# An expert stage written out step by step, with the weight folding spread over the stage before it

## The reference

```python
# attn: 16 heads of 8
q, k, v = xr @ Wq.T, xr @ Wk.T, xr @ Wv.T          # xr = xn by heads
probs = softmax((q * k).sum(-1) / sqrt(128), axis=0)   # over the 16 sequences
attn = probs[..., None] * v.sum(axis=1)[:, None]
# ffn: 16 experts of width 176, top 2, and a shared one of width 352
cw = top-2 weights of softmax(xf @ gate_w + gate_b)
h, g = xf @ w1 + b1, xf @ w3 + b3                  # per expert
y = (silu(h) * g) @ w2, weighted by cw, + cw @ b2
z = silu(xf @ sw1 + sb1) * (xf @ sw3 + sb3) @ sw2 + sb2
out = x + attn + y + z
```

## Time and profile before

| | us |
|---|---|
| median of 3 runs (range) | 261.24 (260.04 to 261.77) |
| the profiled execution | 261.67 |
| its span on the engines | 259.8 |
| first and last scatter to `xslot` start | 34.5, 116.7 |
| first fold of the weights | 109.2 |
| last copy of a fold starts | 126.8 |
| first expert matmul | 129.84 |
| first and last scatter to `ydram` start | 135.60, 236.84 |

### The profile page before, as it was taken

How to read it: one execution, slowest core, us unless ns; L and a number is a source line. 1 busy time by engine, 2 the same in 40 slices (tenths; PEclk the granted TensorE clock), 3 DMA queues, 4 the chain that set the end, 5 groups by cost and what they waited for, 6 DMA issues and landing times.

```text
span 259.8 us, 5535 instructions
## 1 busy us (share of the span) xinstructions
PE 216.3 (83%) x1284; PEld 170.1 (65%) x1285; DVE 185.7 (71%) x525; ACT 115.0 (44%) x331; POOL 151.3 (58%) x170
## 2 busy tenths in 40 slices
PE   0669996799999999999599999999999999990000
PEld 0459943279676655652189999899999999980000
DVE  4898998768765797825747777677777777760495
ACT  2233532831216332224346767676676767750000
POOL 8134058777777777771017777777776777774000
PEclk9999997999999999999979999999999999997555
DMA  5999501446111111110322434343333333311998
GB/s 178 348 383 338 121 29 61 146 141 225 64 58 57 59 57 57 57 59 23 80 57 87 109 112 113 96 116 114 101 110 96 115 109 107 96 51 42 288 395 288
DMA packets 29463, 33.37 MB, mean 128 GB/s; under 512 B 5683, under 2 KB 24627, under 8 KB 29091
## 3 DMA queue, kind: packets, MB, share of 16 engines
q1 hardware_dynamic: 22566, 21.17, 27.9%
q0 software_dynamic: 4576, 9.91, 10.3%
q10 hardware_dynamic: 2304, 2.10, 2.3%
HBM read 18.84 MB, written 14.32 MB: 128 GB/s over the span
## 4 chain that ended last, share of the span: by engine, by line
PE 76%; DVE 8%; DMA 6%; ACT 3%; SPq 3%; issue 2%; POOL 1%; POOLq 0%; ACTq 0%
PE PS L997 15%; PE PS L1016 14%; PE PS L899 8%; PE PS L867 6%; PE PS L868 6%; PE PS L878 4%; PE PS L837 4%; PE PS L1006 4%; PE PS L991 4%; DMA xnT<-ydram 4%; PE PS L1007 3%; SPq L344 3%; PE PS L855 3%; PE PS L830 2%; DVE st L432 2%
## 5 line engine op out<-in xcount | busy, mean ns | idle before, releaser
L419 POOL DMA_INDIRECT ydram<-fw x79 | 75.7, 958 | 44.4 <-DVE fw L703 27.4
L411 POOL DMA_INDIRECT xslot<-XR,idx x64 | 63.5, 993 | 29.5 <-issue 18.0
L1016 PE MATMUL PS<-fw 89*128 (+1 forms) x316 | 49.3, 278 | 0.1
L1016 PEld LDWEIGHTS PS<-fw 89*128 89x128 f32 (+1 forms) x316 | 41.8, 192 | 0.8 <-issue 0.3
L695 DVE TENSOR_TENSOR prod<-prod,PS 128x176 f32<-128x176 f32 x79 | 26.7, 338 | 21.3 <-ACT prod L805 20.8
L805 ACT ACTIVATE prod<-PS 128x176 f32<-128x176 f32 x79 | 25.1, 317 | 18.5 <-PE PS L997 17.9
L997 PE MATMUL PS<-w13h,rxh 128*128 x79 | 32.6, 413 | 0.7 <-DVE rxl L690 0.7
L810 ACT ACTIVATE fw<-PS 88x256 f32<-88x256 f32 x79 | 30.1, 380 | 1.4 <-PE PS L1007 1.0
L703 DVE TENSOR_SCALAR fw<-PS,fw 128x128 f32<-128x128 f32 x79 | 27.7, 350 | 2.8 <-PE PS L1016 2.4
L800 ACT ACTIVATE rxh<-PS 128x128 fp32r<-128x128 f32 x79 | 21.9, 278 | 16.5 <-PE PS L991 16.5
L766 ACT ACTIVATE sS<-PS,sbc 128x512 f32<-128x512 f32 (+1 forms) x18 | 12.2, 686 | 37.5 <-PE PS L868 31.9
(11 more groups left out here) (135 smaller groups left out, 347.0 us busy)
## 6 DMA issues: line engine op xcount, KB each, us to landing
fw<-xslot SPq DMA_DIRECT2D x79, 72.0 KB
fw<-in_w SPq DMA_DIRECT2D x1, 2816.0 KB, 16.0
X<-in_x SPq DMA_DIRECT2D x4, 512.0 KB, 6.2
XR<-ydram SPq DMA_DIRECT2D x8, 256.0 KB, 5.4
out<-X ACTq DMA_DIRECT2D x16, 128.0 KB, 5.3
xnT<-ydram SPq DMA_DIRECT2D x8, 256.0 KB, 7.9
fw<-in_w SPq DMA_DIRECT2D x1, 1536.0 KB, 18.7
ydram<-fw POOLq DMA_INDIRECT x79, 2.2
```

The source lines that it names most:

```text
L411: pool.indirect_dma_start(xslot, bass.IndirectOffsetOnAxis(ap=idx[:, k, t:t + 1], axis=0), XR[:, t, :], None).then_inc(d_sc[k][h], 16)
L419: pool.indirect_dma_start(ydram, bass.IndirectOffsetOnAxis(ap=RX[:, v, TOK:TOK + 1].bitcast(I32), axis=0), yb[:, v, :], None).then_inc(d_y ...
L1016: ins = pe.matmul(PS[:, 6 + b, 0:P], raT[0:n, b, k * P:(k + 1) * P], w2[0:n, bass.ds(e * 2 * P + k * P, P)], start=(k == 0), stop=(k == 1))
```

## The change

Four parts.

1. **Expert steps written out.** `steps` calls `run(j)` for `j` from -1 to 82 on PE, ACT, DVE and POOL. No loop is left there; SP's loads stay a loop.
2. **Folding spread.** The folds move from the end of stage 2 into it, one between two pieces of the shared expert, from after `down(2)` to before `down(5)`. All use bank 5, and each waits for the split of the one before. Their copies (`high`) and splits are put between the `gates` and `gated_up` calls of ACT and DVE. `down` of every group but 1 now writes bank 4 and waits for the `add_z` before it. ACT's wait for the zero fill moves with the first copy.
3. **Bias rows by DMA.** The fold is one matmul of 127 useful rows. The bias row is row 127 (it was row 0; `XR` has its column of ones behind the features instead of ahead). ACT rounds the biases to `bhi`, DVE subtracts to `blo`, SP stores both to DRAM and loads them as row 127 of `w13h` and `w13l`. POOL's five operations that cut the bias in three, and its two for `sel`, go.
4. **Sooner slot loads, other paces.** `KEPT` goes from 8 to 4, and the scatters of the second half wait by new numbers and by a table for folds (`PACE_W`).

The diff, cut to its core (renumbered slices, semaphore names and removed `fixed` arguments left out):

```diff
-WBANK = (0, 2, 1, 3)
-KEPT = 8
+KEPT = 4
+RAW = 8
+WP = P - 1
-PACE_UP = {8: 3, 11: 4, ..., 33: 12, 37: 13, 39: 14, 43: 15, 44: 16, 45: 17, 49: 18, ..., 60: 24}
+PACE_UP = {8: 3, 11: 4, ..., 33: 12, 38: 13, 40: 14, 48: 16, 50: 17, 58: 19, 60: 20}
-PACE_Z = {21: 1, 25: 2, 36: 3, 41: 4, 48: 5, 54: 6, 62: 7}
+PACE_W = {37: 1, 39: 2, 41: 3, 44: 4, 46: 5, 49: 6, 51: 7, 54: 8, 56: 9, 59: 10, 61: 11}
+PACE_Z = {21: 1, 25: 2, 36: 3, 43: 4, 53: 5, 63: 6}
...
-        def steps(eng, run, top=None):
-            turns = (NS - 4) // UN
-            for j in range(-1, 3 + UN):
-                run(j, j, True)
-            with eng.Fori(1, turns) as it:
...
-                for u in range(3, 3 + UN):
-                    run(it * UN + u, u, False)
-            for j in range(3 + turns * UN, NS + 4):
-                run(j, j, True)
+        def steps(run):
+            for j in range(-1, NS + 4):
+                run(j)
...                                                 # SP
-            for k in range(3):
-                sp.dma_start(bdram[k]..., bprt[:, k, :]).then_inc(d_bst, 16)
-            sp.wait_ge(d_bst, 48)
-            sp.dma_start(bsp[:], bdram[:, :]).then_inc(d_bup, 16)
+            for k, part in enumerate((bhi, blo)):
+                sp.dma_start(bdram[k]..., part[:].bitcast(F32)).then_inc(d_bst, 16)
...
+            sp.wait_ge(d_bst, 32)
+            sp.wait_ge(d_fill, 16 + 16 * NE)
+            sp.dma_start(w13h[WP:P, :].bitcast(F32), bdram[0:1, :]).then_inc(d_bup, 16)
+            sp.wait_ge(s_sm, 2 * NB)
+            sp.dma_start(w13l[WP:P, :].bitcast(F32), bdram[1:2, :]).then_inc(d_bup, 16)
...                                                 # ACT, after the copies of group 2
+                    act.wait_ge(l_b, 16)
+                    act.activation(bhi[:], braw[:], ACT.Copy).then_inc(k_bh, 1)
...                                                 # DVE, after norm(7)
+            dve.tensor_tensor(blo[:], braw[:], bhi[:].bitcast(F32), ALU.subtract).then_inc(k_bl, 1)
...                                                 # PE
             def fold(q):
-                if q < 4:
-                    pe.wait_ge(s_sm, NG * NB - 1 + q // 2)
-                else:
-                    pe.wait_ge(s_wl, q - 3)
-                at = PS[:, WBANK[q % 4], 0:WQ]
-                pe.matmul(at, kc[:, K_FOLD:K_FOLD + P], w13[:, cols], start=True, stop=False)
-                pe.matmul(at, sel[:], bsp[:, cols], start=False, stop=True).then_inc(s_w, 1)
+                if q:
+                    pe.wait_ge(s_wl, q)
+                else:
+                    pe.wait_ge(l_w13, 16)
+                    pe.wait_ge(s_za, 2)
+                pe.matmul(PS[:, 5, 0:WQ], kc[:, K_FOLD:K_FOLD + P], w13[:, q * WQ:(q + 1) * WQ],
+                          start=True, stop=True).then_inc(s_w, 1)
             def down(g):
                 if g >= 2:
-                    pe.wait_ge(s_za, g - 1)
+                    pe.wait_ge(s_za, g if g > 2 else 1)
...
```

More of the change, by code:

```diff
@@ L420, in run @@
                                             yb[:, v, :], None).then_inc(d_y[v], 16)
-            steps(pool, run)
+            steps(run)
         @block.vector
@@ L646, in _ @@
             score(7)
+            split(0)
+            shift_scores()
             gated_up(4, 0)
-            shift_scores()
+            split(1)
+            add_z(2)
             gated_up(4, 1)
-            add_z(2)
+            split(2)
+            shares()
+            split(3)
+            add_z(3)
             gated_up(4, 2)
-            shares()
-            add_z(3)
+            split(4)
+            attend(0, True)
             gated_up(5, 0)
-            attend(0, True)
+            split(5)
@@ L656, in _ @@
             gated_up(5, 1)
+            split(6)
             attend(1, True)
+            split(7)
+            add_z(4)
             gated_up(5, 2)
-            add_z(4)
+            split(8)
             attend(2, True)
             gated_up(6, 0)
+            split(9)
+            gated_up(6, 1)
+            split(10)
             attend(3, True)
-            gated_up(6, 1)
+            add_z(5)
             attend(4, True)
             gated_up(6, 2)
-            add_z(5)
+            attend(5, True)
@@ L788, in _ @@
                     gates(g, c)
             act.wait_ge(d_fill, 16 + 16 * NE)
-            for q in range(NW):
-                act.wait_ge(s_w, q + 1)
-                act.activation(w13h[:, q * WQ:(q + 1) * WQ], PS[:, WBANK[q % 4], 0:WQ], ACT.Copy).then_inc(s_wh, 1)
-            def run(j, u, fixed):
-                if has(j + 1, fixed):
-                    b = (u + 1) % 2
+            high(0)
+            act.wait_ge(s_z, 3)
+            gates(4, 0)
+            high(1)
+            act.wait_ge(s_ds, 1)
@@ new lines, in _ @@
+            act.activation(pr[:].rearrange("p c r -> p (c r)"), sd[:].rearrange("p c r -> p (c r)"), ACT.Exp,
+                           scale=float(P) ** -0.5).then_inc(s_exa, 1)
+            gates(4, 1)
+            high(2)
+            high(3)
+            gates(4, 2)
+            high(4)
+            act.wait_ge(s_z, 4)
+            gates(5, 0)
+            high(5)
+            gates(5, 1)
+            high(6)
+            high(7)
+            gates(5, 2)
+            high(8)
+            act.wait_ge(s_z, 5)
@@ L798, in run @@
+            gates(6, 0)
+            high(9)
+            gates(6, 1)
+            high(10)
+            gates(6, 2)
+            act.wait_ge(s_z, 6)
+            for c in range(NB):
+                gates(7, c)
+            def run(j):
+                if has(j + 1):
+                    b = (j + 1) % 2
                     act.wait_ge(r_tp, j + 2)
-                    act.wait_ge(r_up, max(j, 0) if fixed else j)
+                    act.wait_ge(r_up, max(j, 0))
                     act.activation(rxh[:, b, :], PS[:, b, 0:P], ACT.Copy).then_inc(r_xh, 1)
-                if has(j, fixed):
-                    b = u % 2
+                if has(j):
+                    b = j % 2
@@ L810, in run @@
                     act.activation(raT[0:FH, b, :], PS[0:FH, 4 + b, 0:2 * P], ACT.Copy).then_inc(r_att, 1)
             act.wait_ge(k_r1, 1)
-            steps(act, run)
+            steps(run)
             for c in range(NC):
@@ L1020, in _ @@
             read_expert(0, 0)
-            steps(pe, run)
+            steps(run)
 def constants():
```

197 lines of the change are left out of this document (92 added, 105 removed).

## The result

The changed kernel takes 253.26 us (median of 4 runs, 252.61 to 254.27), the kernel before 260.99 (4 runs, 260.04 to 261.77). The ratio is 0.971, 95% interval 0.967 to 0.975. The prediction was 253.5 us.

A forecast was written before the change was run, and what follows sets the result against it. PE and POOL were taken to bound the expert loop at once, so the last scatter plus an untouched tail sets the time. 261.67 - 4.3 - 1.3 - 2.6 = 253.5 us, range 251.0 to 257.0.

The forecast's parts named there:

- Term 1, folds and start-up: First fold to first expert matmul: PE's 20.7 us become 16.4 with one-matmul folds spread out, 4.3 us sooner.
- waits of folds for splits: In the shared expert, PE's waits between folds for the split before: 2.2 us, between 0 and 5.6.
- That leaves over 4 us for the first load.: Expert-stage start: last scatter to xslot lands at 119.0, PE's first transpose comes at about 124.4, so slot loads are in time.
- The rival of the scatter stream: POOL's 64 scatters to xslot stretch by over 4 us, slot loads come 1 to 3 us late: 254.5 to 256.5; chance 0.05.
- Term 2, the clock: Head of the expert stage: granted clock stays full instead of 0.50 for 3.4 us, worth 1.3 us, between 0 and 1.66.
- Term 3, the turns: Expert loop: writing out the steps removes POOL's extra idle time at five loop turns, 2.6 us sooner, between 0 and 2.7.
- The clock did not fall at the start-up: Rival: clock falls all the same, as holes of 0.9 us around down(7) might count together; 254.8 us, chance 0.15.
- ACT and DVE did not bind: Rival: ACT and DVE bound the shared expert, which grows by 5.6 us in place of 2.2; 256.9 us, chance 0.10.
- the turns were the cause: Rival said they were not: a loss only coinciding with expert-loop turns stays, 0.5 us goes; 255.6 us, chance 0.07.
- Code: Rival: PE starves for code in the written-out steps, some 8 more packets, 9.6 us lost; 263 us, chance 0.03.
- the tail: From the last scatter at 236.84 to the end at 261.67: 24.8 us, which the change does not touch.
- The edits at nothing: Bias operations off POOL, rounding and subtraction on ACT and DVE, SP's bias loads, ACT's moved zero-fill wait: no cost or gain.

The follow-up runs named there:

- the version with filler: Written-out steps, one-matmul folds at the end, attend(7) ahead of the last splits, unused matmuls in PE's two long idle times: 252.29 us, 0.967 of the kernel before.

## Why the prediction was right, and where it was right by luck

**Term 1, folds and start-up: -4.3 forecast, -4.82 measured.** Of it 0.60 came from ahead of the folds and 4.22 from the work that the term is about: 23.51 + 29.10 us before, 8.05 + 40.34 after. In detail (forecast, measured): folds 9.5, 9.5; waits of folds for splits 2.2, 1.8 (40.34 - 29.10 - 9.46); hole before `down(7)` 0.9, 1.0; `down(7)` to the first expert matmul 1.1, 1.7. The last is 0.5 over because of the step that failed:

**"That leaves over 4 us for the first load."** It left none. The sum was made with the last scatter starting at 116.7 as before; it started at 118.75 and had landed at 121.01. SP's first load went out at 121.87, and the two transposes started 2.85 and 3.61 us after the landing, where PE was free after 2.35. The 2 us are a start later by 1.07 and a scatter of 2.39 us, neither an effect of the new paces: with the loop kept, the same paces have the last scatter at 115.75, and with `down(7)` in bank 5 at 116.37. But the scatter of 2.39 us is no accident of one execution. It is in eight of the fourteen traces, at the same place of the stream, 13.9 us after its start; here it is in the kernel before with its steps written out:

```profile
48.27 2.39 POOL L402 DMA_INDIRECT xslot<-XR,idx  x1 [0.30 <-issue]
```

All eight are among the nine traces in which the clock stays at 1.00 at 42 us; none of the five in which it falls has it. The gain at 42 us and this loss on POOL mostly come together. In the change the slow scatter stands beside three DVE operations on `sS` (L544, 48.84 to 50.71), as one of 1.30 us at 53.46 does (52.63 to 54.52); whether they hold it isn't shown. The rival of the scatter stream thus came true in a small part, 0.5 us of the 1 to 3 that I gave it. A margin taken from one execution was less sure than the durations taken from it. With the hole before `down(7)` gone and the loads in time, the same piece is 1.3 us (123.19 to 124.49), near the 1.1 forecast.

**What the 0.6 us beyond the term are: luck.** Two effects that I did not have work against each other ahead of the folds. A part of the input landed later, which puts POOL's first scatter and PE behind it 1.07 us later, and the clock did not fall at 42 us:

```profile
43.15 0.27 PE L856 MATMUL PS<-mbf,lbf 128*128 128x256 bf16 x1 [1.29 <-DVE cum L495]
```

PE's idle time is 1.29 us here for 2.00 in the earlier trace rows, and the clock stays at 1.00 behind it, where 3.3 us at half had cost up to 1.7. The traces of four changed kernels still have that spell, and the kernel before with only its steps written out doesn't have it, so this gain is not a property of the change.

**What I gave the term to was wrong in part.** The prediction treats shorter folds and spread folds as one term. The experiment with the folds at the end splits it: 4.0 us for the shorter fold, 0.3 for the spreading, and the version with filler gets there sooner with no spreading (18.48 us for 19.29). What spreading did save is the idle time that costs the clock, which is the second term's account and not this one's. The rows said as much without my seeing it: PE is busy in every microsecond of the shared expert, so moving 9.5 us of PE work there frees nothing but waits.

**Term 2, the clock: -1.3 forecast, -1.28 measured.** First expert matmul to first scatter is 4.48 us for 5.76, at a clock of 1.00. What I read off holds: idle times of 0.9 us and less at the start-up cost no clock, and 3.32 us did, for 6.8 us. The price has a second witness in 17 runs of the kernel before: nine with a mean clock of 0.947 or more have a median of 260.0 us, eight with 0.943 or less 261.2. A spell of 3.3 us at half is 0.006 of the mean clock, which is what the two groups differ by, so I take the 1.2 us for the price of one spell. No run of either group has a trace; the traced run of the kernel before, at 0.943, has the spell at 42 us, which is another place than the term's.

**Term 3, the turns: -2.6 forecast, -2.40 measured**, and shown by two experiments: 2.2 us back in the time with the loop restored, 2.4 us gone in the trace of the kernel before without it. One idle time of 0.55 us stays.

**The rivals.** The clock did not fall at the start-up; ACT and DVE did not bind (waits of 1.8 us for the 5.6 of that rival); the turns were the cause. Code: 12 packets where I had some 15, and PE busy for 64.00 of 64.00 us in the steps, so none of them stopped it. The rule of the Trainium skill ("Runtime: NRT & Kernel Launch", Instruction fetch mechanics) that straight code is fetched ahead of its use is cited for it, and the trace agrees.

**The sum:** 4.82 + 1.28 + 2.40 = 8.50 us for 8.2, and the tail is 24.88 us for 24.83. Without the 0.60 from ahead of the folds the terms give 7.9, so the forecast came out as near as it did partly by luck, well inside its range either way. The edits at nothing cost nothing that the trace shows.

## What to carry to other kernels

Where an engine is busy in every microsecond of a stretch, moving its own work into that stretch wins at most the waits at the old place, and pays the waits at the new one; what wins is making the work shorter. Before relieving one engine of a loop, read the pace of each: where two stand at the same height, either relief alone is nearly worthless (1.0 and 0.2 us), and both together are not (7.7 us). A margin between two streams that one execution shows as 4 us can be gone in the next, so a forecast that needs it should carry it as a cost with a chance.

## What the runs showed of the hardware

- TensorE's idle time before the routing's cumulative sums, at 42 us, differs from kernel to kernel: after 0.92, 1.29, 1.35, 1.44, 1.58 and 1.62 us the granted clock stayed 1.00; after 1.85, 2.00, 2.18, 2.30 and 2.35 us it fell to about 0.50 for some 3 us. After 3.32 us of idle in another place it fell for 6.8 us. A short spell costs 1.2 us in this kernel, by my estimate from 17 runs. With unused matmuls in the idle time the clock stayed 1.00 in all three traces that have them, and six runs of one such kernel have a mean clock of 0.951 to 0.956.
- A turn of a 12-step loop costs 0.5 us on the path with four engines looping in step (101.2 us for 98.8 with five turns), and up to 1.0 us at one of them.
- POOL issues an indirect DMA of 128 rows every 0.96 + 0.30 us when nothing else holds it. Some of the 64 to `xslot` take 1.0 to 1.4 us, and one of them took 2.39 us in eight of fourteen traces, all of them traces with the clock at 1.00 at 42 us.
- One chip ran every kernel 50 us slower with instructions of the same length, by stops of all its engines every 5.4 us. There the change won 0.9% instead of 2.9%.
